# First attention of a two-layer kernel: plain q and k, head pairs in row and column groups, select after exp

## The reference, cut to what matters

```python
qkv = jnp.einsum('btc,oc->bto', x, W_qkv).reshape(B, T, 3, H, D)
q = q * cos + _rotate_half(q) * sin        # k alike
q = _rms_norm(q)                           # k alike
scores = jnp.einsum('bhqd,bhkd->bhqk', q, k) * scale
scores = jnp.where(causal[None, None], scores, jnp.float32(-1000000000.0))
attn = jax.nn.softmax(scores, axis=-1)
out = jnp.einsum('bhqk,bhkd->bhqd', attn, v)
return jnp.einsum('btc,oc->bto', out, W_o)
```

## Time and profile before

| what | value |
|---|---|
| runs | 2547.64, 2548.65, 2553.36 us, median 2548.65 |
| the profiled execution | 2547.07 us, its span 2545.3 us |
| mean granted PE clock | 0.936 |
| PE busy | 2254.1 us, 89% |
| VectorE, ScalarE, GpSimd busy | 1478.7, 933.9, 847.2 us (58, 37, 33%) |
| DMA | 131.42 MB, 52 GB/s over the span |
| the values' matmuls of the first attention (L512) | 1280 records, 151.6 us |

### The profile page before, as it was taken

One profiled execution on the slowest core, in us unless ns is written; L12 is line 12 of the kernel. 1 busy time (PEld: TensorE's weight loads), 2 busy tenths in 40 slices (PEclk: granted clock), 3 DMA queues, 4 the chain that ended last, 5 costly groups with the idle time before them and its releaser, 6 DMA issues. The chain is left out here.

```text
span 2545.3 us, 30676 instructions
## 1 busy us (share of the span) xinstructions
PE 2254.1 (89%) x10674; PEld 1499.8 (59%) x10674; DVE 1478.7 (58%) x2330; ACT 933.9 (37%) x1814; POOL 847.2 (33%) x1241
## 2 busy tenths in 40 slices
PE   6998556998999888997999888997999988899999
PEld 3865443954956444774677544495486744478444
DVE  4755895655334896563533599464543479756322
ACT  1421761721412761540332465162141266245000
POOL 4454364515300254521620055251540015442000
PEclk9999567989999899998999899998999999999899
DMA  4334000010112010201103010201010301020121
GB/s 186 135 115 161 0 1 0 2 54 7 70 50 75 25 50 7 85 1 55 75 1 112 13 47 28 91 2 56 0 75 1 124 4 46 25 92 1 75 75 42
DMA packets 19560, 131.42 MB, mean 52 GB/s; under 512 B 1856, under 2 KB 1856, under 8 KB 14528
## 3 DMA queue, kind: packets, MB, share of 16 engines
q1 hardware_dynamic: 19392, 129.28, 13.9%
HBM read 116.42 MB, written 12.85 MB: 51 GB/s over the span
## 5 line engine op out<-in xcount | busy, mean ns | idle before, releaser
L754 PE MATMUL ps<-XET,ring 128*128 128x512 f32 x1024 | 464.6, 603 | 0.0
L1563 POOL TENSOR_TENSOR Y<-Y,HC 128x1024 f32<-128x1024 f32 x120 | 282.8, 2358 | 361.3 <-DVE HC L1097 361.3
L754 PEld LDWEIGHTS ps<-XET,ring 128*128 128x128 f32 x1024 | 194.8, 195 | 217.9 <-issue 217.7
L1086 DVE TENSOR_TENSOR_SCAN HS<-DA,ps 128x1024 f32<-128x1024 f32 x128 | 291.9, 2281 | 31.3 <-ACT DA L1410 27.4
L772 PE MATMUL ps<-ring,GE 128*128 128x512 f32 x512 | 242.5, 613 | 47.7 <-DVE ACC L1125 40.6
L1531 POOL TENSOR_TENSOR STK<-QN,STK 128x128 fp32r<-128x128 f32 x512 | 235.2, 485 | 144.4 <-ACT STK L1348 134.1
L1504 POOL TENSOR_SCALAR RS<-MV 128x1 f32<-128x1 f32 x64 | 21.9, 343 | 559.6 <-DVE MV L818 559.6
L1410 ACT ACTIVATE DA<-DL,AN 128x511 f32<-128x511 f32 x256 | 170.2, 712 | 89.5 <-DVE HS L1086 89.4
L772 PEld LDWEIGHTS ps<-ring,GE 128*128 128x128 f32 x512 | 96.1, 194 | 159.0 <-issue 147.8
L434 PE MATMUL ps<-ring,XNT 128*128 128x512 f32 x384 | 171.1, 604 | 10.2 <-ACT V L1352 10.2
L1225 DVE TENSOR_REDUCE NMX<-ps 128x1 f32<-128x128 f32 (+3 forms) x256 | 124.7, 488 | 88.5 <-PE ps L692 88.0
(11 more groups left out here) (176 smaller groups left out, 3955.9 us busy)
## 6 DMA issues: line engine op xcount, KB each, us to landing
ring<-experts_dram SPq DMA_DIRECT2D x32, 1536.0 KB, 6.8
tern<-tern_q SPq DMA_DIRECT2D x33, 768.0 KB, 4.4
RAW<-tern_dram SPq DMA_DIRECT2D x22, 768.0 KB, 5.1
ring<-wqkv_dram SPq DMA_DIRECT2D x4, 3072.0 KB, 13.6
tern_q<-tern SPq DMA_DIRECT2D x11, 768.0 KB, 7.3
pack<-pack_dram SPq DMA_DIRECT2D x1, 4432.0 KB, 17.9
X<-x_dram SPq DMA_DIRECT2D x4, 1024.0 KB, 5.8
out_dram<-ACC SPq DMA_DIRECT2D x3, 1024.0 KB, 5.1
```

Source lines behind the costliest of these rows:

```text
L754: last = pe.matmul(ps[:, e_banks(e)[n]], ring[:, e_slot(e), c:c + P], XET[:, k], start=(k == 0), stop=(k == NK - 1))
L1086: v.tensor_tensor_scan(HS[:, q].rearrange("p j t -> p (j t)"), DA[:, q].rearrange("p j t -> p (j t)"), ps[:, 2 * q:2 * q + 2].rearrange("p ...
L1563: p.tensor_tensor(y, y, HC[:, q], ALU.add).then_inc(c_y, 1)
```

## The change

- q and k are no longer stacked. Each token tile of QN is transposed as it is (`pe_A_qk`, eight transposes), ScalarE copies q to QT, VectorE k to KT. All of it lies in the lead-in.
- Scores in f32 with 32 contraction rows. Two heads make a pair and lie in different row groups (`heads_of`); eight pairs instead of 16 heads. The mask matmuls go.
- One exp covers a piece of both heads. Then GpSimd puts zeros above the diagonal in PT (`p_A_select`, two `affine_select` of 2 and 6 blocks of 128 columns per pair), and the values wait for that.
- For the values V is the stationary operand, 32 columns of V beside 32 of ones (VA), PT the moving one; the pair's heads lie in column groups 0 to 63 and 64 to 127 of the output. The result has channels along the partitions, and 32 equal rows of the denominator.
- `v_A_pair`: two reciprocals of 32x512 from PSUM and two products of 32x512 straight into AOT. The head transposes and their copies go.
- In the first block four absolute sums stand in the rotation loop, seven between the pairs; the thresholds are formed before the last pair is divided.
- VA lies where the ternary chunks 0 and 1 go, so their loads wait for the last values of the attention.

```diff
-          + [(("stack", 0, g, i), "dve") for g in range(NG) for i in range(NT)]
-          + [(("heads", 0, i), "act") for i in range(NT)]
+          + [(("qk", i, z), ("act", "dve")[z]) for i in range(NT) for z in range(2)]
...
+        def pe_project_A(pe):
+
+            pe.wait_ge(a_head, NP)
+            for i in range(NT - 1):
+                pe_project_tile(pe, wo, i)
+            pe_norm(pe, 1, 0)
+            pe_project_tile(pe, wo, NT - 1)
+            pe_norm(pe, 1, 1)
...
-                        pe_stack(pe, 0, 0, j)
-            pe_stack(pe, 0, 0, NT - 1)
...
+                        pe_A_qk(pe, j)
+            pe_A_qk(pe, NT - 1)
+            for z in range(2):
+                t_emptied(pe, ("qk", NT - 1, z))
+            pe.wait_ge(v_copied, NT)
+            for p in range(NP):
+                pe_A_scores(pe, p)
+                if p:
+                    pe_A_pv(pe, p - 1)
+            if not experts:
+                pe.wait_ge(abs_sums, 1)
+                pe.wait_ge(a_exp, 3 * NP)
+                pe.matmul(ps[:, 7, 0:3], ONES[:], SABS[:], start=True, stop=True).then_inc(thr_sum, 1)
+            pe_A_pv(pe, NP - 1)
...
+        def heads_of(p):
+
+            g, o = divmod(p, 2)
+            return [(4 * g + r, slice(32 * r, 32 * r + 32)) for r in (o, o + 2)]
+
+        def pe_A_scores(pe, p):
+            for unit, (_, col, width) in enumerate(A_UNIT):
+                if p:
+                    pe.wait_ge(a_exp, 3 * (p - 1) + unit + 1)
+                for kt in (k for k in range(NT) if A_PLACE[k][0] == unit):
+                    off = A_PLACE[kt][1] - col
+                    for x, (h, rows) in enumerate(heads_of(p)):
+                        last = pe.matmul(ps[:, 2 + 2 * unit + x, off:off + T - kt * P], KT[rows, h // 4, tile(kt)],
+                                         QT[rows, h // 4, kt * P:T], start=True, stop=True)
+                last.then_inc(a_scores, 1)
+
+        def v_ones(h, kt):
+
+            return VA[:, kt, h // 2, h % 2:h % 2 + 2].rearrange("p a d -> p (a d)")
+
+        def pe_A_pv(pe, p):
+            if p == 0:
+                pe.wait_ge(ones_a, 1)
+            pe.wait_ge(a_sel, p + 1)
+            if p >= 2:
+                pe.wait_ge(a_head, p - 1)
+            for kt in range(NT):
+                for x, (h, _) in enumerate(heads_of(p)):
+                    col = A_PLACE[kt][1]
+                    last = pe.matmul(ps[64 * x:64 * x + 64, p % 2, kt * P:T], v_ones(h, kt),
+                                     PT[:, p % 2, x, col:col + T - kt * P], start=(kt == 0), stop=(kt == NT - 1),
+                                     skip_group_check=True)
             last.then_inc(a_pv, 1)
...
+        def v_A_pair(v, p):
+
+            v.wait_ge(a_pv, p + 1)
+            odd = p % 2
+            for h, rows in heads_of(p):
+                den = slice(rows.start + 32 - 64 * odd, rows.stop + 32 - 64 * odd)
+                v.reciprocal(RA[rows], ps[den, odd]).then_inc(a_recip, 1)
+            v.wait_ge(a_recip, 2 * p + 2)
+            for h, rows in heads_of(p):
+                ins = v.tensor_tensor(AOT[rows, h // 4], ps[rows, odd], RA[rows], ALU.mult)
+            ins.then_inc(a_head, 1)
...
+                if i < NT and not experts:
+                    v_abs_sums(v, i)
+            for i in range(NT):
+                t_copy(v, v.tensor_copy, ("qk", i, 1), KT[:, :, tile(i)])
+            for p in range(NP):
+                if p:
+                    v_A_pair(v, p - 1)
+                if not experts and NT + p < NM:
+                    v_abs_sums(v, NT + p)
+            if not experts:
+                v.wait_ge(abs_parts, 3 * NM)
+                v.tensor_reduce(SABS[:], SPART[:], AX.X, ALU.add).then_inc(abs_sums, 1)
+                v_thresholds(v)
+            v_A_pair(v, NP - 1)
...
+        def p_A_select(p, n):
+
+            p.wait_ge(a_exp, 3 * (n + 1))
+            square = PT[:, n % 2].rearrange("p x (k q) -> p (x k) q", q=P)
+            for blocks in (square[:, 7::12], square[:, 0:21:4]):
+                ins = p.affine_select(blocks, blocks, [[0, blocks.shape[1]], [1, P]], ALU.is_ge, 0.0, base=0, channel_multiplier=-1)
+            ins.then_inc(a_sel, 1)
...
-                        for m in range(3):
-                            load_tern(sp, m)
                         sp.wait_ge(v_done, NT)
                         for e in range(1, 4):
                             load_expert(sp, e)
+                        sp.wait_ge(a_pv, NP)
+                        for m in range(3):
+                            load_tern(sp, m)
```

## The result

The changed kernel takes 2580.28 us, median of four runs (2579.58 to 2581.24), where the kernel before, run beside it, takes 2548.14. The ratio is 1.012, 95% interval 1.0105 to 1.0134. The profiled execution took 2580.4 us against 2547.07. So the change costs some 32 us; 2566 (+17) was forecast, in a range of 2530 to 2645.

A forecast was written before the change was run, and what follows sets the result against it. VectorE's reciprocals were to bound the attention at 7.8 us per pair. Three loop blocks at +0.8 (+2.4) and the first block's +14.8 gave +17.2 on 2547.07, or 2564.3; 2566 us as median, range 2530 to 2645.

The forecast's parts named there:

- The mechanism: Attention: two 3.2 us reciprocals and two products cost VectorE 7.8 us per pair, over PE's 5.3, so VectorE bounds.
- Rival 5: Attention: a still slower reciprocal, 4.4 us, makes a pair 10.2 us; +77, 2643 us; chance 0.06.
- Overlap on PE: Attention: a pair's two heads run side by side, scores 2.7 us and values 2.6, 5.3 a pair instead of 8.6.
- Rival 1: Attention: no overlap on PE, 8.6 us per pair, PE bounds loop blocks; 2583 us; chance 0.17.
- Rivals 2 and 3: Attention: cheap reciprocal; with overlap on PE 2461 us, chance 0.19; without overlap 2552 us, no change, chance 0.07.
- granted clock of 1.00: Attention: the forecast expected PE's granted clock to stay at 1.00.
- rival 4: Attention: PE's clock falls, 8.3 to 10.6 us per pair; 2580 to 2645 us, middle 2605; chance 0.06.
- The attention's size: From first scores to projection: 72.1 us where it was 68.5, +3.6 per block.
- the select: GpSimd in the attention: 3.1 us per pair, hidden in the period but delaying the first pair.
- The absolute sums: First block, between pairs: seven more on VectorE, six on the path, 11.2 us.
- The lead-in: Before the first scores: 4 us less waiting, 2.1 more transposes; -1.9 per loop block, 0 in the first.
- The tail: After the projection starts: two groups of head transposes of 0.43 us go, -0.9 per block.

The follow-up runs named there:

- e1_copy: The changed kernel with both reciprocals of a pair replaced by copies of the same shape, division left out: 2446.72 us.
- e6_serial: e2_one with value matmuls, and the scores' two-key-tile piece, issued head after head instead of alternating between a pair's heads: 2504.68 us.
- e11_rows: e2_one with the scores of both heads of a pair computed from the first head's rows, so in one row group: 2590.34 us.
- e4_order: The changed kernel with the last pair's values moved ahead of the thresholds' matmul in the first block: 2572.96 us.
- e2_one: The changed kernel with one reciprocal of 128x512 per pair instead of two of 32x512: 2466.39 us.
- e12_six: The changed kernel with the edits of e2_one and e4_order, and six projection matmuls issued before the last pair is divided: 2445.02 us.
- e3_loads: The kernel before with only the three ternary loads moved behind the experts' loads and the first attention's last values: 2547.36 us, ratio 0.9976.
- e8_shift: The kernel before with the first block's small thresholds matmul issued 25 times instead of once: 2559.51 us, ratio 1.0030.
- e9_early: The changed kernel with the edits of e2_one and e4_order, and twelve projection matmuls issued before the last pair is divided: 2453.42 us.

## Why the prediction was right, and where it was off

**The mechanism held.** VectorE's reciprocal bounds the attention, PE waits for its product, and its size from a four-element instruction (3.2 us) was near the measured 3.35. e1_copy shows that nothing else holds the period near 8.2: with copies it drops to 4.66. By itself: the Trainium skill (VectorE: DVE Perf Modes, First, the fixed hardware budget) gives the reciprocal a repeat count of 8; the two sizes here give (3353 - 182)/(512 - 4) = 6.2 ns per column, six of the 1.04 ns columns of a plain read, not eight. Rival 5 (4.4 us) falls by the measured 3.35.

**Overlap on PE** was right: 2.43 and 2.37 us for 2.7 and 2.6, shown by e6_serial (values) and e11_rows (scores). Rival 1 falls. Rivals 2 and 3 fall with the 3.35 us. The forecast's granted clock of 1.00 was wrong: it was 0.77 to 0.81, as in rival 4. Yet it didn't set the period, since only the values ran slowly between the pairs, and slow values with the scores behind them took 4.06 + 2.43 us at most in the loop block shown, under 8.2. It cost at the two ends, before the first product and in the projection.

**The attention's size was short.** Forecast +3.6 per loop block, measured +7.4, +6.2, +6.8. Of the first loop block's 3.8 too few, 3.2 are the pair (8.20 for 7.8, eight times: 0.15 per reciprocal and 0.12 between instructions), the rest the start: the first reciprocal came 10.35 us after the first scores, not 9.6, since the first values ran at the lowered clock (3.93 for 2.6); a part of that was given back by the select, 1.23 us where 3.1 was taken.

**The absolute sums** are on the path as forecast; VectorE, first block:

```profile
94.08 6.74 DVE L906 RECIPROCAL RA<-ps 32x512 f32<-32x512 f32 x2
100.85 1.39 DVE L909 TENSOR_TENSOR AOT<-ps,RA 32x512 f32<-32x512 f32 x2
102.27 1.87 DVE L992 TENSOR_REDUCE SPART<-RAW 128x1 f32<-128x512 f32 x3
104.18 3.35 DVE L906 RECIPROCAL RA<-ps 32x512 f32<-32x512 f32 x1
```

The period is 10.1 us there. The block's +21.4 for 15.7 is again the pair, 3.2, and most of 3.26 us that the forecast didn't see: it priced the thresholds as 0.9 us on VectorE and didn't ask what stood behind their matmul in PE's queue. There stood the last values, which VectorE then waited for (e4_order).

**The lead-in failed:** -1.9 forecast, +0.7 to +0.9 measured. I let PE's 4 us of waiting go and added 2.1 for transposes. The wait shrank by only 2.6 us (2.56 + 2.73 us of gaps before the last V matmuls, 2.7 after), since the new transposes wait for VectorE's copies of k, and V's last matmuls ran slow:

```profile
653.69 1.09 PE L507 MATMUL ps<-pack,QN 128*128 128x128 f32 x8 [1.94 <-DVE KT L884]
655.14 1.11 PE L507 MATMUL ps<-pack,QN 128*128 128x128 f32 x4 [0.35 <-DVE KT L884]
656.04 4.79 PE L452 MATMUL ps<-ring,XNT 128*128 128x512 f32 x8
```

4.79 us at a granted clock of 0.75, for what took 3.60 before. So -2.6 + 2.1 + 1.2 = +0.7. The first block, with four absolute sums in this loop, took 2.9 more, where I had chosen 0 between -1.9 and +2. These parts are read from the trace and weren't tried by themselves.

**The tail:** -0.9 forecast, 0 measured. The two groups of transposes went, but the matmuls after PE's 11.76 us of waiting are slower still: from the first of them to the first addition to X 6.37 us (738.45 to 744.82), before 5.41 (703.52 to 708.93). That wait is 7.2 us with one reciprocal (e2_one), and 2.34 in e12_six.

**The boundaries:** nothing forecast, -13 in all measured. The loads' part is tried (e3_loads: 2.0 and 1.3 us); for the rest the place in PE's instruction list is the likely cause (e8_shift). Without this luck the change would have cost some 46 us for the +17 that was forecast: the mechanism was right, but that the number came as near as it did is partly chance. The sum was thus saved by errors of opposite sign: 11 us of lead-ins, 15 of attention and 4 of tails too few, 13 of boundaries and 3 ahead of the second attention too many. The last (-2.8 between ternary matmuls and second attention in two blocks) is the clock of the experts' down projection: 13.59 us there in e2_one and e12_six as in the changed kernel, 15.3 in e9_early, 16.45 or 15.22 in e3_loads. Why the clock falls there in one kernel and not in another stays open.

## What to carry to other kernels

Price an elementwise operation of VectorE by its columns, whatever the number of partitions (32 and 128 took the same here): a denominator laid along the free axis costs 512 columns of a slow function, so take it once for all partitions, the unneeded ones too. When one engine becomes the bound, look at what lies behind each wait in the queues around it: the last pair's values and the projection were both free to go first. And before a gain at a far place is put down to an edit, shift the instruction list alone, and compare the granted clock there.

## What the runs showed of the hardware

- A f32 reciprocal from PSUM takes 3353 ns for 32x512 and 3358 for 128x512; 170 to 184 for 128x4. A product of 32x512 whose inputs lie in different partitions (one in PSUM, one in SBUF) takes 687 ns, as with both in the same.
- The granted clock fell while PE's records left no gap. The three-column matmuls of e8_shift stand one behind the other for 7.30 of 7.30 us at 0.75 on the mean, then the 13.5 us of ordinary work behind them run at 0.50; twenty value records take 4.46 us for 2.3:

```profile
120.00:129.00 9.00, 9.00 (x81) 8.44 (x80) 6.65 (x16) 4.98 (x16) 3.39 (x8) 1.00 0.54 193
129.00:136.30 7.30, 7.30 (x53) 7.30 (x51) 1.13 (x2) 0.03 (x1) 0.00 (x0) 0.75 0.01 2
136.50:150.00 13.50, 13.50 (x62) 12.30 (x62) 1.56 (x9) 2.94 (x6) 8.34 (x6) 0.50 0.01 1
```

- Scores in one row group (e11_rows) ran 32 us at 0.66 with PE never idle; in two row groups (e2_one) the attention of a loop block got 0.91 in all and 1.00 from 645 to 680.
- In the kernel before PE stands 6.27 and 6.04 us in the middle of equal matmuls at the two boundaries where its loop jumps back, and nowhere in the router of the first and last sequence. 24 more matmuls ahead of the loop removed that (one run). A wait of 5.6 to 7.2 us before the router stayed in both.
